# One AdaLN transformer block on one core: the second norm's chain and five engines' order within a step

## Chip, cores and metric

One NeuronCore of a Trainium2 chip (trn2) runs the whole program. The metric is device time in microseconds (us), of single executions; three of them are shown for the kernel before, with their median. One more execution was taken with the profiler, and all rows come from that one.

## What is computed

Eight batch rows of 1024 tokens with 256 channels go through two blocks, each with a layer norm, a modulation that depends on the row, and a gate on the residual. The first block is a causal linear attention over Chebyshev features, the second a mixture of eight experts with the top two chosen, plus one shared expert.

```python
def _layernorm(x, axis=-1, eps=1e-05):
    m = jnp.mean(x, axis=axis, keepdims=True)
    v = jnp.var(x, axis=axis, keepdims=True)
    return (x - m) / jnp.sqrt(v + eps)
...
    # attention: Tq, Tk are Chebyshev features of clipped q, k
    Tv = Tk * v[:, :, :, None, :]
    kv_prefix = jnp.cumsum(Tv, axis=2)
    ks_prefix = jnp.cumsum(Tk.sum(axis=-1), axis=2)
    num = (Tq * kv_beta).sum(axis=3)
    den = (Tq.sum(axis=-1) * k_beta).sum(axis=3)
    out_h = num / (den[..., None] + EPS_DEN)
    return jnp.einsum('bsd,ed->bse', out, W_out)
...
    # experts
    activation = jnp.sqrt(jax.nn.softplus(logits))
    top_vals, top_idx = jax.lax.top_k(activation, K)
    hdn = jax.nn.silu(jnp.einsum('nd,edh->enh', Xf, rW1) + rb1[:, None, :])
    y = jnp.einsum('enh,ehd->end', hdn, rW2) + rb2[:, None, :]
    routed = jnp.einsum('ne,end->nd', cf, y).reshape(B, T, d)
    return shared + routed
...
h = _layernorm(x, axis=-1) * (1 + ca) + sa
x = x + ga * _L0_attn_ref(h, L0_attn_W_in, L0_attn_W_out)
h = _layernorm(x, axis=-1) * (1 + cb) + sb
x = x + gb * _L0_ffn_ref(h, ...)
```

## The kernel before

The work is cut into 16 chunks of 512 tokens, two to a batch row: chunk (i, p) is half p of row i. The program is a software pipeline of steps, one per chunk, written out by hand for each engine (the `step` functions; a loop over rows 2 to 6 or 1 to 6, the first and last steps unrolled). In step (i, p) four chunks are in work at once: the first norm of the chunk two ahead, the query, key and value projections of the next chunk, the attention of chunk (i, p), the second norm and routing of the chunk before it (called prev), and the experts of the chunk two back. Each engine executes its list strictly in order, and semaphores join the lists.

The parts that the change and the prediction speak of, by engine:

- VectorE (`step` at L1191, in the block that begins at L957). `residual` (L1090) adds x to the output of W_out; `token_stats` (L368) takes the second norm's statistics with `bn_stats`; `odd` (L977) makes the third and fifth order features; `lows` (L961) makes a low part, the rounding rest of a normalised chunk, from PSUM, the high part and the modulation (n = 0 for the first norm, n = 1 for the second); `weigh` (L994) multiplies values by key features, `prefix` (L1010) is the prefix sum over tokens, `order_product` (L1032) multiplies by query features. Orders come in the sequence 0, 1, 3, 4, 2, so the fourth order product is that of order 4 and the fifth that of order 2. `logit_parts` (L1099) ranks the experts, `softplus` (L1126) and `combine_weights` (L1152) make the two weights of a token. `den_key_sums` and `den_products` make the denominators' terms, `invert` (L1069) takes the reciprocal, `finish_numerator` (L1076) adds the last order, `divide` (L1083) multiplies by the inverse that has been spread over the channels, and `weigh_hidden` (L1164) multiplies an expert's hidden layer by its weight.
- GpSimd (`step` at L738). `inv_std(pool, 1, ...)` (L346) turns the second norm's statistics into an inverse deviation and a shift, in ten small instructions. `weigh_order_5` (L648) makes the fifth order's weighted values; `scale_wo` (L716) scales W_out by the gate of the row, in p = 0 steps; `add_orders` (L655) issues a DMA that adds one order's product onto another in SBUF. The first (n = 0) waits for two order products, the second (n = 1) for four, the last (n = 2) for the landing of both. `exps` and `scores` are powers for the softplus and the square root, `split_weights` (L684) cuts the combine weights into bf16 parts.
- SyncE (`step` at L600) issues the other DMAs: `spread_inverse` (L572) writes the inverse denominators to DRAM (L576) and, when they are there, reads them back spread over the partitions (L581); `spread_weights` does the same for the combine weights; `load_gate` (L568) fetches a row's gate.
- ScalarE (`step` at L863): `highs` makes the high parts from PSUM, `normalise_second` applies the second norm, `scale_even` scales two query features, `copy_qkv` and `hidden` empty PSUM (the latter with SiLU), `combine_rows` copies the transposed combine weights.
- TensorE (`step` at L1503): `transposes`, `project`, `route_logits`, `logits_by_token`, `head_sums`, the nine experts, `denominators`, `project_out` (W_out) and `combine_by_expert`, the transposes of the combine weights.

What sets the order around the change is only the sequence of the calls in these five lists and the waits in front of each instruction. The last sum's wait is

```python
if n < 2:
    pool.wait_ge(products, ND * c + 2 * n + 2)
else:
    pool.wait_ge(added[0], 16 * c + 16)
    pool.wait_ge(added[1], 16 * c + 16)
```

## Time and profile before

| what | us |
|---|---|
| three runs | 957.63, 956.96, 951.9 |
| their median | 956.96 |
| the profiled execution | 953.07 |
| its span, first to last instruction | 951.3 |
| TensorE matmuls busy | 860.2 (90%) |
| VectorE busy | 815.7 (86%) |
| ScalarE busy | 489.8 (51%) |
| GpSimd busy | 408.3 (43%) |

Of the span, some 85 us are the setup and the first step, and the last 70 us are two steps with experts alone. In between the steps follow each other at 52 to 54 us. A timeline's row gives the start and the length of a group of like instructions, and in square brackets the idle time of the engine ahead of it with what ended that; an instruction that is much longer than its like was held while it ran.

### The profile page before, as it was taken

To read this page: it belongs to the slowest core of one execution; us is meant where nothing else is said; L and a number is where in the kernel's file an instruction comes from. 1 tells how busy PE (TensorE), PEld (TensorE's weight loads), DVE (VectorE), ACT (ScalarE), POOL (GpSimd) and SP (SyncE) were. 2 spreads that over 40 slices of the span, in tenths; PEclk is the share of its full clock that TensorE was granted. 3 is DMA by queue.
4 is the path that set the end of the run, shared out by engine and by line. 5 is a ranking of instruction groups with operands and counts; after the bars stand their busy time and mean duration, and the time that the engine had idled before them with its cause. 6 is when DMAs were issued, how large, how long until landed. Compare 5 with 4: busy or idle time off the path is not lost. (4 is left out here: it accounts for less than half of the span.)

```text
span 951.3 us, 14272 instructions
## 1 busy us (share of the span) xinstructions
PE 860.2 (90%) x4377; PEld 648.6 (68%) x4377; DVE 815.7 (86%) x1263; ACT 489.8 (51%) x860; POOL 408.3 (43%) x502
## 2 busy tenths in 40 slices
PE   5766739999999999999999999999999999979998
PEld 4545427676767676786767676777767676756786
DVE  2696979999989998999989998999999998889423
ACT  4634546555556656655656566566556563441321
POOL 2341444363636355453636254543646253463220
PEclk9975769999999999999999999999999999999999
DMA  8014134453533535453534445354634243443422
GB/s 309 1 29 89 45 68 145 86 153 76 137 92 77 153 79 160 86 155 70 153 77 96 130 87 165 68 155 90 162 71 133 66 100 113 78 133 83 117 79 55
DMA packets 51705, 100.34 MB, mean 105 GB/s; under 512 B 5380, under 2 KB 34127, under 8 KB 49623
## 3 DMA queue, kind: packets, MB, share of 16 engines
q1 hardware_dynamic: 36356, 66.14, 21.2%
q0 software_dynamic: 14832, 33.03, 20.2%
q10 hardware_dynamic: 482, 0.74, 0.2%
q8 instruction: 18, 0.29, 0.1%
q14 instruction: 17, 0.13, 0.0%
HBM read 57.68 MB, written 17.06 MB: 79 GB/s over the span
## 5 line engine op out<-in xcount | busy, mean ns | idle before, releaser
L1487 PE MATMUL acc<-w,hid 128*128 128x256 f32 x1128 | 262.5, 380 | 2.6 <-DVE hid L1169 2.6
L1487 PEld LDWEIGHTS acc<-w,hid 128*128 128x128 f32 x1128 | 213.9, 190 | 37.6 <-DVE hid L1169 4.7
L845 ACT ACTIVATE hid<-ring,b1row 128x512 f32<-128x512 f32 x144 | 98.7, 685 | 143.0 <-PE ring L1368 140.4
L1169 DVE TENSOR_TENSOR hid<-hid,cfw 128x512 f32<-128x512 f32 x128 | 111.1, 870 | 37.0 <-DMA cfw<-cf_rows 21.6
L665 POOL DMA_DIRECT2D feat<-feat x48 | 43.7, 910 | 228.8 <-DVE feat L1046 115.0
L800 ACT ACTIVATE feat<-ring,bqkv 128x512 f32<-128x512 f32 x96 | 65.7, 686 | 81.9 <-PE ring L1368 81.9
L1368 PE MATMUL ring<-n2H,w1H 128*128 128x512 f32 x288 | 102.5, 437 | 0.0
L1445 PE MATMUL tr<-wo_g,feat 128*128 128x256 f32 x256 | 65.3, 413 | 35.9 <-DVE feat L1088 35.9
L1021 DVE TENSOR_TENSOR_SCAN feat<-zero,carry,feat 128x512 f32<-128x512 f32 x80 | 97.1, 1261 | 0.0
L1021 DVE TENSOR_TENSOR_SCAN feat<-zero,feat 128x512 f32<-128x512 f32 x80 | 95.7, 1243 | 0.0
L1368 PE MATMUL ring<-n2H,w1L 128*128 128x512 f32 x288 | 90.8, 397 | 0.0
L1368 PE MATMUL ring<-n2L,w1H 128*128 128x512 f32 x288 | 90.5, 395 | 0.0
L1421 PE MATMUL tr<-feat,const 128*32 128x512 f32 x640 | 89.1, 602 | 0.0
L1445 PEld LDWEIGHTS tr<-wo_g,feat 128*128 128x128 f32 x256 | 51.6, 207 | 49.2 <-DVE feat L1088 33.7
L1368 PE MATMUL ring<-n1H,winH 128*128 128x512 f32 x192 | 69.5, 444 | 15.2 <-issue 7.9
L820 ACT ACTIVATE feat<-feat,const 128x1024 f32<-128x1024 f32 x64 | 70.2, 1142 | 1.0
L353 POOL TENSOR_TENSOR ms<-stats 128x4 f32<-128x4 f32 x18 | 30.2, 1678 | 88.4 <-DVE stats L378 88.4
L1368 PEld LDWEIGHTS ring<-n2H,w1L 128*128 128x128 f32 x288 | 54.4, 189 | 12.7
L1368 PEld LDWEIGHTS ring<-n2L,w1H 128*128 128x128 f32 x288 | 54.5, 189 | 12.5
L1368 PE MATMUL ring<-n1H,winL 128*128 128x512 f32 x192 | 62.8, 409 | 0.0
L1368 PE MATMUL ring<-n1L,winH 128*128 128x512 f32 x192 | 62.8, 409 | 0.0
L1368 PEld LDWEIGHTS ring<-n2H,w1H 128*128 128x128 f32 x288 | 48.8, 191 | 18.5 <-issue 11.7
(171 smaller groups left out, 1559.8 us busy)
## 6 DMA issues: line engine op xcount, KB each, us to landing
feat<-feat POOLq DMA_DIRECT2D x48, 512.0 KB, 4.6
cfw<-cf_rows SPq DMA_DIRECT2D x16, 1280.0 KB, 7.6
xin<-in_L_attn_x SPq DMA_DIRECT2D x16, 512.0 KB, 9.3
feat<-inv_rows SPq DMA_DIRECT2D x32, 256.0 KB
cfw<-cf_rows SPq DMA_DIRECT2D x16, 512.0 KB, 3.6
out<-x SPq DMA_DIRECT2D x15, 512.0 KB, 8.5
out<-fin POOLq DMA_DIRECT2D x15, 512.0 KB, 6.0
cfw<-cf_rows SPq DMA_DIRECT2D x16, 256.0 KB, 4.5
```

Of the source, the lines that this page charges most:

```text
L353: nc.gpsimd.tensor_tensor(t(1), m0, m1, ALU.subtract).then_inc(mv_steps[n], 1)
L665: g.dma_start(f(into), f(of), accum_op=ALU.add).then_inc(added[n], 16)
L800: a.activation(feat[:, (K0 + p, Q0 + p, V0)[m // 2], m % 2], ring[bank][:, :], ACT.Identity, bias=col(bqkv[:, (2, 3, 0, 1, 4, 5)[m]], i)). ...
L820: a.activation(f((qa, qb)[which - 1]), f(s), ACT.Square, bias=cv["biases"][:, which - 1:which]).then_inc(squares, 1)
L845: a.activation(hid[:, e % NG], ring[bank][:, :], ACT.Silu, bias=b1row[:, e:e + 1]).then_inc(ring_copied, 1)
L1021: last = v.tensor_tensor_scan(feat[:, W + n, h], zero[:, 0:1].to_broadcast([P, CT]), feat[:, W + n, h], carry[:, n, h:h + 1] if p else 0.0 ...
L1169: v.tensor_tensor(hid[:, e % NG], hid[:, e % NG], cfw[:, (e - 1) % NW], ALU.mult).then_inc(hidw_ready, 1)
L1368: last = mm(out, w, x, start=(n == 0), stop=(n == len(terms) - 1))
L1421: last = mm(tr[q][g_ * QS:(g_ + 1) * QS, :], cv["headsum"][:, (r // HPH) * QS:(r // HPH + 1) * QS], feat[:, srcs[n], h], start=(n < 4 and ...
L1445: last = mm(tr[t // 2][:, (t % 2) * D:(t % 2 + 1) * D], attn[:, k, t * P:(t + 1) * P], wo_g[:, k], start=(k == 0), stop=(k == KD - 1))
L1487: last = mm(acc[t // 2][:, t % 2], hid[:, e % NG, t * P:(t + 1) * P], w2[:, e], start=False, stop=(e == E), skip_group_check=True)
```

## The change

Every edit changes the order of calls, apart from the second norm's statistics, which get a new path. The lists in words:

- Second norm: VectorE finishes mean and variance itself (`bn_aggr` and two small instructions), and GpSimd keeps a power and a multiplication.
- VectorE: first low part right behind the statistics, second low part ahead of the first prefix sum, logit parts behind expert 3, softplus behind the denominators, combine weights ahead of the reciprocal.
- GpSimd: the order-5 product waits for the second weighted value; the powers of the routing move ahead of the second and of the last order sum, the first norm's inverse deviation to the end.
- ScalarE: the second norm's four normalisations and high part ahead of the key and query copies, the combine rows ahead of the first norm's normalisation.
- TensorE: the two norms' transposes, routing and token logits sooner, head sums later, the combine transposes ahead of W_out.
- SyncE: the gate for W_out is fetched at the end of the row before.

```diff
+        def second_mean_var(dve, i, p):
+
+            c = number(i, p)
+            dve.wait_ge(stats_ready[1], c + 1)
+            dve.sem_inc(aggregate_begun, 1)
+            for t in range(NT):
+                last = nc.vector.bn_aggr(mean_var[:, t], stats[:, 1, t])
+            last.then_inc(aggregated, 1)
+            dve.wait_ge(aggregated, c + 1)
+            nc.vector.tensor_scalar(ms[:, 1, 8], mean_var[:, :, 1], EPS_LN, None, ALU.add).then_inc(mean_var_ready, 1)
+            nc.vector.tensor_scalar(ms[:, 1, 10], mean_var[:, :, 0], -1.0, None, ALU.mult).then_inc(mean_var_ready, 1)
+
+        def second_inv_std(pool, i, p):
+
+            c = number(i, p)
+            pool.wait_ge(mean_var_ready, 2 * c + 2)
+            ge(pool, norm_ready[1], c)
+            nc.gpsimd.tensor_tensor(ms[:, 1, 9], ms[:, 1, 8], k_("-half", NT), ALU.pow).then_inc(second_pow, 1)
+            pool.wait_ge(second_pow, c + 1)
+            nc.gpsimd.tensor_tensor(ms[:, 1, 11], ms[:, 1, 10], ms[:, 1, 9], ALU.mult).then_inc(rstd_ready[1], 1)
...
             def step(i, p, gb, loads):
                 if p == 0:
-                    if loads or i < B:
-                        ge(sp, wo_ready, i)
-                        load_gate(i, 0)
+                    if i == 0:
+                        load_gate(0, 0)
...
+                if p == CB - 1 and i + 1 < B:
+                    sp.wait_ge(wo_ready, i + 1)
+                    load_gate(i + 1, 0)
...
                 ge(pool, numerator, c)
+                pool.wait_ge(weighted, (ND - 1) * c + 2)
                 g.tensor_tensor(f(W + 4), f(KT5), f(V0), ALU.mult).then_inc(weighted5, 1)
...
-                    inv_std(pool, 1, *later(i, p, -1))
+                    second_inv_std(pool, *later(i, p, -1))
...
-                if st["attn"]:
-                    add_orders(i, p, 1)
-                if st["norm"]:
-                    inv_std_of_squares(pool, *later(i, p, 2))
                 if st["second"]:
                     exps(*later(i, p, -1))
                 if st["attn"]:
+                    add_orders(i, p, 1)
+                if st["second"]:
+                    scores(*later(i, p, -1))
+                if st["attn"]:
                     add_orders(i, p, 2)
                 if st["second"]:
-                    scores(*later(i, p, -1))
                     split_weights(*later(i, p, -1))
+                if st["norm"]:
+                    inv_std_of_squares(pool, *later(i, p, 2))
...
                 silu(0)
-                silu(1)
                 if qkv:
                     highs(0, *nxt)
+                if second:
+                    for t in range(NT):
+                        normalise_second(act, *prev, t)
+                silu(1)
                 silu(2)
                 if attn_:
                     scale_even(i, p)
-                for t, half in enumerate(HALVES[:4]):
-                    copy(half)
-                    if second:
-                        normalise_second(act, *prev, t)
-                silu(3)
                 if second:
                     highs(1, *prev)
-                silu(4)
+                for half in HALVES[:3]:
+                    copy(half)
                 if second:
                     copy_logits(*prev)
+                copy("q1")
+                silu(3)
+                silu(4)
...
                 silu(8)
+                if second:
+                    combine_rows(*prev)
...
-                if second:
-                    combine_rows(*prev)
...
                     token_stats(dve, 1, *prev)
+                    second_mean_var(dve, *prev)
+                if qkv:
+                    lows(0, *nxt)
                 if attn_:
                     odd(i, p, 1)
                     weigh(i, p, 0)
-                if qkv:
-                    lows(0, *nxt)
+                    weigh(i, p, 1)
+                if second:
+                    lows(1, *prev)
...
-                if second:
-                    lows(1, *prev)
-                if attn_:
                     order_product(i, p, 0)
                     order_product(i, p, 1)
                 expert(3)
+                if second:
+                    logit_parts(*prev)
...
                     order_product(i, p, 2)
                     order_product(i, p, 3)
-                if second:
-                    logit_parts(*prev)
-                if attn_:
                     den_key_sums(i, p)
                     den_products(i, p)
+                if second:
+                    softplus(*prev)
...
                 expert(5)
                 if second:
-                    softplus(*prev)
+                    combine_weights(*prev)
                 if attn_:
                     invert(i, p)
...
                 if ffn:
                     expert_up(*exp, use, 0)
+                if qkv:
+                    transposes(0, *nxt)
+                if ffn:
                     expert_up(*exp, use, 1)
                     second_biases(*exp)
...
                 expert(0)
-                if qkv:
-                    for half in HALVES[:4]:
-                        project(*nxt, use, half)
-                expert(1)
                 if second:
                     transposes(1, *prev, behind_norm=qkv)
-                expert(2)
+                if qkv:
+                    for half in HALVES[:3]:
+                        project(*nxt, use, half)
                 if second:
                     route_logits(*prev)
+                if qkv:
+                    project(*nxt, use, "q1")
+                if second:
+                    logits_by_token(*prev)
+                expert(1)
+                expert(2)
...
                 expert(8)
+                if second:
+                    combine_by_expert(*prev, attn_)
...
                 if attn_:
                     project_out(i, p)
-                if second:
-                    combine_by_expert(*prev, attn_)
```

VectorE around the third and fourth order product, before, in step (7, 0); the same sequence stands in every step with both norms. L1008 is a weighted value, L1021 the prefix sums of two orders, L1169 expert 4, L1042 and L1046 the two order products, L1107 to L1113 the beginning of the logit parts:

```order
L1008 TENSOR_TENSOR feat<-feat 128x1024
L1021 SCALAR_TENSOR_TENSOR feat<-zero,feat 128x512 x4
L1169 TENSOR_TENSOR hid<-hid,cfw 128x512
L1030 COPY carry<-feat 128x4
L1042 TENSOR_TENSOR feat<-feat 128x1024
L1046 SCALAR_TENSOR_TENSOR feat<-feat 128x1024
L1107 TENSOR_REDUCE route<-misc 128x32
L1111 TENSOR_TENSOR prod<-route 128x256
L1113 MAX top<-route 128x8 x4
```

The same place after the change (lines are 30 higher there):

```order
L1147 SCALAR_TENSOR_TENSOR best<-top 128x8
L1149 TENSOR_SCALAR best<-top 128x8
L1152 TENSOR_TENSOR prod<-prod,const 128x256
L1154 TENSOR_REDUCE route<-prod 128x32
L1038 TENSOR_TENSOR feat<-feat 128x1024
L1051 SCALAR_TENSOR_TENSOR feat<-zero,feat 128x512 x4
L1199 TENSOR_TENSOR hid<-hid,cfw 128x512
L1060 COPY carry<-feat 128x4
L1072 TENSOR_TENSOR feat<-feat 128x1024
L1076 SCALAR_TENSOR_TENSOR feat<-feat 128x1024
L1086 SCALAR_TENSOR_TENSOR prod<-const,tr 128x512
```

The logit parts have moved from behind the two order products to ahead of the weighted value; the denominators' prefix sum (L1086) follows the products.

VectorE at the beginning of the same step, before: residual (L1096), statistics (L378), odd features (L984, L986), weighted values (L1002, L1004), first low part (n1L), prefix sums:

```order
L1096 TENSOR_TENSOR x<-tr,xin 128x512 x2
L378 BN_STATS stats<-x 128x6 x4
L984 SCALAR_TENSOR_TENSOR feat<-feat 128x1024
L986 SCALAR_TENSOR_TENSOR feat<-feat 128x1024
L1002 TENSOR_TENSOR feat<-feat 128x1024
L968 SCALAR_TENSOR_TENSOR n1L<-tr,mods,n1H 128x512 x2
L1004 SCALAR_TENSOR_TENSOR feat<-feat 128x1024
L1021 SCALAR_TENSOR_TENSOR feat<-zero,feat 128x512 x2
L1169 TENSOR_TENSOR hid<-hid,cfw 128x512
L1004 SCALAR_TENSOR_TENSOR feat<-feat 128x1024
L1169 TENSOR_TENSOR hid<-hid,cfw 128x512
L1021 SCALAR_TENSOR_TENSOR feat<-zero,feat 128x512 x2
```

And after it, to the second low part:

```order
L1126 TENSOR_TENSOR x<-tr,xin 128x512 x2
L381 BN_STATS stats<-x 128x6 x4
L390 BN_AGGR mean_var<-stats 128x2 x4
L393 TENSOR_SCALAR ms<-mean_var 128x4
L394 TENSOR_SCALAR ms<-mean_var 128x4
L998 SCALAR_TENSOR_TENSOR n1L<-tr,mods,n1H 128x512 x2
L1014 SCALAR_TENSOR_TENSOR feat<-feat 128x1024
L1016 SCALAR_TENSOR_TENSOR feat<-feat 128x1024
L1032 TENSOR_TENSOR feat<-feat 128x1024
L1034 SCALAR_TENSOR_TENSOR feat<-feat 128x1024
L998 SCALAR_TENSOR_TENSOR n2L<-tr,mods,n2H 128x512 x2
```

Before, the second low part stands one small copy behind these twelve rows, after two pairs of prefix sums, three weighted values and two experts; now only the aggregation, the first low part and four products lie between the statistics and it.

GpSimd from the order-5 product (L653) to the weights' split (L698), before. L723 is W_out's scaling, the L665 are the three order sums, L672 the power of the softplus, L681 the scores:

```order
L653 TENSOR_TENSOR feat<-feat 128x1024 [waits numerator,odd_ready]
L723 TENSOR_TENSOR wo_g<-wo,gates 128x512 [waits projected,ga_loaded]
L665 DMA feat<-feat 128x1024 [waits order_products] x2
L672 TENSOR_TENSOR best<-pool_c,best 128x8 [waits softplus_steps,logit_parts]
L665 DMA feat<-feat 128x1024 [waits orders_added0,orders_added1]
L681 TENSOR_TENSOR best<-best,pool_c 128x8 [waits combine_weight_steps,softplus_steps]
L698 TENSOR_TENSOR part<-split,pool_c 128x32 [waits combine_transposed,combine_weight_steps]
```

And after it:

```order
L680 TENSOR_TENSOR feat<-feat 128x1024 [waits values_weighted,numerator,odd_ready]
L750 TENSOR_TENSOR wo_g<-wo,gates 128x512 [waits projected,ga_loaded]
L692 DMA feat<-feat 128x1024 [waits order_products]
L699 TENSOR_TENSOR best<-pool_c,best 128x8 [waits softplus_steps,logit_parts]
L692 DMA feat<-feat 128x1024 [waits order_products]
L708 TENSOR_TENSOR best<-best,pool_c 128x8 [waits combine_weight_steps,softplus_steps]
L692 DMA feat<-feat 128x1024 [waits orders_added0,orders_added1]
L725 TENSOR_TENSOR part<-split,pool_c 128x32 [waits combine_transposed,combine_weight_steps]
```

The softplus power stands ahead of the second sum and the scores ahead of the last one; the order-5 product has one more wait.

## Rows read from the trace of the kernel before

**Rows 1.** Busy time by stretch, divide to divide: length, then each engine; clock, DMA.

```profile
403.16:455.02 51.86, 50.53 (x266) 38.46 (x266) 49.99 (x75) 30.19 (x55) 23.51 (x30) 1.00 0.45 112
...
455.02:508.31 53.29, 51.11 (x267) 38.38 (x267) 49.87 (x80) 30.48 (x57) 26.36 (x30) 1.00 0.46 114
```

**Rows 2.** VectorE's timeline, one p = 1 step: start, us, instructions, [idle before <-releaser].

```profile
413.82 1.41 DVE L968 SCALAR_TENSOR_TENSOR n1L<-tr,mods,n1H 128x512 fp32r<-128x512 f32 x2
...
418.65 2.83 DVE L1169 TENSOR_TENSOR hid<-hid,cfw 128x512 f32<-128x512 f32 x1
...
426.49 1.41 DVE L968 SCALAR_TENSOR_TENSOR n2L<-tr,mods,n2H 128x512 fp32r<-128x512 f32 x2 [0.91 <-ACT n2H L788]
...
438.26 1.21 DVE L1046 SCALAR_TENSOR_TENSOR feat<-feat 128x1024 f32<-128x1024 f32 x1
...
439.40 0.21 DVE L1107 TENSOR_REDUCE route<-misc 128x32 f32<-128x64 f32 x1
...
439.99 0.37 DVE L1113 MAX8 top<-route 128x8 f32<-128x8 f32 x4
...
441.45 1.28 DVE L1056 TENSOR_TENSOR_SCAN prod<-const,kcarry,tr 128x512 f32<-128x512 f32 x1
...
455.02 1.34 DVE L1088 TENSOR_TENSOR feat<-feat 128x512 f32<-128x512 f32 x2 [0.38 <-DMA feat<-inv_rows]
```

**Rows 3.** GpSimd's timeline, the same step.

```profile
414.84 1.04 POOL L363 TENSOR_TENSOR ms<-ms,pool_c 128x4 f32<-128x4 f32 x1
...
417.51 3.42 POOL L653 TENSOR_TENSOR feat<-feat 128x1024 f32<-128x1024 f32 x1
...
440.06 0.87 POOL L665 DMA_DIRECT2D feat<-feat  x1 [6.96 <-DVE feat L1046]
...
445.15 0.91 POOL L665 DMA_DIRECT2D feat<-feat  x1 [0.38 <-issue]
...
447.30 1.66 POOL L681 TENSOR_TENSOR best<-best,pool_c 128x8 f32<-128x8 f32 x1 [1.24 <-DVE best L1150]
```

**Rows 4.** SyncE's queue, the end of the same step.

```profile
447.88 0.62 SPq L576 DMA_DIRECT2D inv_rows<-denom  x1
...
450.06 1.21 SPq L581 DMA_DIRECT2D feat<-inv_rows  x2
```

**Rows 5.** GpSimd's timeline, the end of the last attention step (7, 1).

```profile
868.12 0.91 POOL L665 DMA_DIRECT2D feat<-feat  x1 [2.53 <-issue]
```

**Rows 6.** SyncE's queue there.

```profile
869.71 0.63 SPq L576 DMA_DIRECT2D inv_rows<-denom  x1
...
873.06 1.21 SPq L581 DMA_DIRECT2D feat<-inv_rows  x2
```

**Rows 7.** ScalarE's timeline in step (7, 1): SiLU, one of two scalings, four normalisations.

```profile
837.69 0.69 ACT L845 ACTIVATE hid<-ring,b1row 128x512 f32<-128x512 f32 x1 [1.57 <-PE ring L1368]
...
838.28 1.05 ACT L828 ACTIVATE feat<-feat 128x1024 f32<-128x1024 f32 x1
...
845.83 2.07 ACT L435 ACTIVATE ntok<-x,ms 128x256 f32<-128x256 f32 x4 [5.56 <-POOL ms L366]
```

**Rows 8.** VectorE's timeline, the next step (p = 0): expert 2, second low part.

```profile
472.42 2.67 DVE L1169 TENSOR_TENSOR hid<-hid,cfw 128x512 f32<-128x512 f32 x1 [0.26 <-DMA cfw<-cf_rows]
...
479.76 1.41 DVE L968 SCALAR_TENSOR_TENSOR n2L<-tr,mods,n2H 128x512 fp32r<-128x512 f32 x2 [2.22 <-ACT n2H L788]
```

**Rows 9.** GpSimd's timeline there: W_out's scaling.

```profile
479.56 1.29 POOL L723 TENSOR_TENSOR wo_g<-wo,gates 128x512 f32<-128x512 f32 x1 [5.02 <-DMA gates<-gate_rows]
```

**Rows 10.** TensorE's timeline: W_out of steps (7, 0) and (7, 1).

```profile
826.75 5.41 PE L1445 MATMUL tr<-wo_g,feat 128*128 128x256 f32 x16 [2.07 <-DVE feat L1088]
...
879.69 3.72 PE L1445 MATMUL tr<-wo_g,feat 128*128 128x256 f32 x16 [2.35 <-DVE feat L1088]
```

**Rows 11.** Busy time by stretch, the first of these two.

```profile
826.70:832.00 5.30, 5.25 (x16) 4.24 (x17) 4.07 (x6) 0.00 (x0) 1.57 (x2) 0.68 0.32 31
```

**Rows 12.** Who waited for whom: us in total, times, longest.

```profile
DVE n2L L968 <- ACT n2H L788: 24.8, 16, 3.6
```

22 lines of the change are left out of this document (9 added, 13 removed).

## Prediction

> **What bounds the kernel now.** I looked first at the stretches from one divide to the next, one step each. The two shown last 51.86 and 53.29 us; TensorE is busy for 50.53 and 51.11 us of them and VectorE for 49.99 and 49.87 [rows 1]. Two engines are full at once, so busy shares decide nothing and the question is which chain closes the loop. The step ending at 455.02 stands for a second half row (p = 1), the next for a first one (p = 0); the kernel has six of the one kind and seven of the other between the divides at 137.35 and 825.36, which last 52 to 54 us.
>
> Next I read VectorE's own timeline [rows 2]. The divide at 455.02 waited for the spread of the inverse denominators (0.38 us, DMA), so VectorE's own work is not what ends there. Following that wait back over three queues gives a chain with fixed links. The fourth order product (438.26) ends at 439.40. GpSimd issues the second order sum at 440.06, the last order sum at 445.15 [rows 3]; SyncE writes the inverse at 447.88, issues its spread at 450.06 [rows 4], and the spread lands as the divide starts at 455.02. So the divide comes 15.62 us after the fourth order product: 0.66 + 5.09 + 4.91 + 4.96.
>
> The third link is the one to look at twice: is it the small write that takes 2.18 us (447.88 to 450.06), or does the spread wait until the last sum is through? In the last attention step the last sum is issued at 868.12 [rows 5] and the write at 869.71, so the write is 1.2 us nearer to the sum than before; the spread goes at 873.06 [rows 6]. The write now took 3.35 us, and the distance from sum to spread is 4.94, the same as 4.91. I read this as: the write is held until the last sum has gone through. The second link is of the same kind: in the code the last sum waits for the second to land.
>
> The Trainium skill, DMA: Bandwidth & Descriptors, Queues, rings and completion order, says that each DMA engine goes round between the queues it has work for, packet by packet; by that rule a small write would not wait for a whole transfer from another queue. The same section says that a semaphore's increment lands only after all earlier writes of that engine across its queues, which is what the 3.35 us look like. The first rule is a rival below.
>
> **The change, part by part.** I count to the end of the fourth order product, which was 36.24 us after the divide (403.16 to 439.40), and add the chain behind it.
>
> What leaves VectorE ahead of that point in a p = 1 step: the wait for the second norm's high part, 0.91 us, and a stall: weighted values of order 5 on GpSimd (3.42 us at 417.51) held VectorE's product at 418.65 for 2.83 instead of the usual 0.68, so 2.15 [rows 2, 3]. The change makes GpSimd start that product only behind the second weighted value, so that it runs while VectorE waits for, or makes, the low part. Low parts read PSUM and were not held by GpSimd: the one at 413.82 took its 1.41 us beside GpSimd's power at 414.84, and the one at 426.49 as long. Together 3.06 us go. In the p = 0 step shown they are 2.22 for the high part and 0.26 + 1.99 at the held product [rows 8]: 4.47.
>
> What comes in ahead of that point. Four aggregations and two small instructions: no row shows the aggregation; four MAX of eight elements took 0.37 us together [rows 2], which bounds it below, and 1.5 would be four times as much; with two small ones I take 0.75, near the MAX. The logit parts move from behind the fourth product to ahead of it: 439.40 to 441.45, 2.05 us, and VectorE is in order, so every order product and both GpSimd sums behind them are that much later. Third, a wait at the low part, which now stands six instructions behind the statistics. Its chain from the statistics' end: 0.75, the power 1.04 and a multiplication on GpSimd with their hand-overs 1.4, four normalisations 2.07, two SiLU at about 0.6, two scalings of the query features (1.05 each, partly overlapped: 1.95), which ScalarE now does ahead of the high part, 0.65 for its first half: 8.1 us with the hand-overs [rows 3, 7]. VectorE has 0.75 + 1.33 + four products at 1.14 = 6.65 us to do meanwhile. Wait: 1.45; bounds 0 (ScalarE free sooner) and 2.9 (the power held up by VectorE's products, as GpSimd's small instructions were). For p = 0, W_out's scaling on GpSimd, 1.29 us at 479.56 [rows 9], which ran beside a low part, now follows the order-5 product and meets a prefix sum; I take 1.0, bounds 0 and 1.3.
>
> Behind that point the chain stays 15.62, plus what GpSimd adds: the scores' power (1.66 us at 447.30) now stands ahead of the last sum. Today it starts 5.85 us behind the logit parts (441.45 to 447.30), with two clips and a weighted product of about 0.6 each between, which now follow it; so it can start some 4 us behind the fourth product and ends 5.7 behind it, just as the second sum lands (0.66 + 5.09 = 5.75). I take 0.15 more; 0 to 0.6, which is one clip.
>
> Sum for p = 1: -3.06 + 0.75 + 2.05 + 1.45 + 0.15 = +1.3 us. For p = 0: -4.47 + 0.75 + 2.05 + 1.45 + 1.0 + 0.15 = +0.9. VectorE does less behind the point, but it then waits longer at the divide: work taken out there buys nothing.
>
> Six steps at 1.3 and seven at 0.9 make 14.1. The ends: step (0,0) has no second norm, but its first low part now stands ahead of four products and waits for the high part; 0 to 4 us, I take 1.5. Step (0,1) by the p = 1 sum: +1.3. Step (7,1) has the longest wait of all for the high part, 3.6 us [rows 12]. It has no first low part to fill the time, so the power stands behind a product (1 us more) and only 0.75 + 4.56 us of work lie beside a chain of 9.1: the wait comes back as 3.8, no stall goes, and 0.75 + 2.05 + 0.2 = +3.0 stay. The last two steps: the combine rows start earlier, against TensorE idle between transposes, routing and token logits; 0, bounds -2 and +2. All in all 14.1 + 1.5 + 1.3 + 3.0 = 19.9.
>
> Costed at nothing: TensorE's new order (it gains a wait of about 0.7 for a key copy that now follows the high part, but has 2 us to spare ahead of W_out); the combine transposes ahead of W_out (their GpSimd work follows the combine weights, which now end before the inverse is written, 7 us ahead of the divide); the gate's load a step sooner (GpSimd's next instruction waits for order products anyway); GpSimd's ten small instructions that become two (they end in the chain above).
>
> The profiled execution took 953.07 (span 951.3): 953.07 + 19.9 = 973.0. The median of the runs is 956.96, so a measured figure may lie up to 4 us higher.
>
> **Rivals.**
> The write is not held, by the round rule above. Then the spread follows the write by 2.18 us. The write moves from 8.48 to 7.2 us behind the fourth product (less 2.05, plus combine weights and their wait for the scores, 0.8), and the divide to 7.2 + 2.18 + 4.96 = 14.35, 1.4 less than my 15.77. Steps become -0.1 and -0.5, the ends 1.5 - 0.1 + 1.6; together -1: 952, no change. Against it stand the 3.35 us [rows 6]; for it, that in the loop's steps write and sum end so close together that they don't tell.
>
> Faster: the chain is free as above and VectorE's new wait of 1.45 does not come, because ScalarE has the high part ready. Then VectorE needs 36.24 - 3.06 + 0.75 + 2.05 + 14.35 = 50.3 us and TensorE becomes the bound, at about 50.8 + 0.5 = 51.25 for both kinds: -0.6 x 6 - 2.0 x 7 = -17.6, with 2 for the ends 937. It decides as soon as the divide leaves less than 14 us behind the fourth product. The busy 50.53 and 51.11 [rows 1] show that floor.
>
> Slower still: TensorE idles 2 to 3 us ahead of W_out in every step, and its clock drops. After 2.07 us of idle that product took 5.41 us at a granted clock of 0.68, towards the lower level of 1.2 GHz; after 2.35 us elsewhere it took 3.72 [rows 10, 11]. If it falls in each of 13 steps, the residual waits 1.5 more: 973 + 19 = 992.
>
> **How the numbers follow.** Forecast 973, chance 0.52, own range 960 to 985. No change (952) 0.22, faster (937) 0.16, clock (992) 0.10. The range of 943 to 986 leaves out the lower part of the third and the upper of the fourth. A measurement tells about 1% from no change: faster 0.2 (the third case and a little of the second), within 0.26, slower 0.54.
>
> **What would show it.** Right: the last sum to the spread stays at 4.9; the fourth product 37 us or more behind the divide; VectorE waiting about 2 us for the inverse's spread at each divide; the held product back to 0.68; a wait of 1 to 2 us at the second low part. Wrong: the spread following the write by 2.2 us with the last sum still under way, or steps at 51 us with TensorE never waiting ahead of W_out.

## The result, and the profile after

The changed kernel takes 991.1 us (median of four, 989.7 to 994.4) against 954.4 for the kernel before (median of four, 951.6 to 957.6): a ratio of 1.0388, with a 95% interval of 1.0338 to 1.0438. The forecast was 973 and its range ended at 986. The profiled execution took 994.4 us with a span of 992.7, so it can be set against the 951.3 of before stretch by stretch, though it was the slowest of the four. From the starts of the 16 divides in each trace (the last column is an experiment, below, and its profiled execution was the fastest of its four, so the last two columns lie further apart than the medians do):

| us | before | changed | a_warm6 |
|---|---|---|---|
| to the first divide | 84.4 | 90.0 | 85.5 |
| step (0, 1) | 53.0 | 52.5 | 51.7 |
| six p = 1 steps, mean | 52.0 | 53.8 | 53.4 |
| seven p = 0 steps, mean | 53.7 | 56.3 | 55.0 |
| step (7, 1) | 52.8 | 56.2 | 54.7 |
| behind the last divide | 73.1 | 76.8 | 73.9 |
| span | 951.3 | 992.7 | 970.7 |

Busy time by stretch in the changed kernel, one p = 1 step and the p = 0 step behind it (columns as in [rows 1]):

```profile
421.01:474.25 53.24, 51.01 (x266) 38.39 (x266) 48.76 (x82) 29.91 (x55) 19.65 (x21) 1.00 0.43 109
474.25:530.85 56.60, 53.37 (x266) 39.44 (x266) 50.02 (x85) 30.11 (x55) 21.09 (x22) 0.97 0.44 108
```

VectorE is busy for less of its step than before and the steps are longer: time went into waiting. TensorE's clock, 1.00 in both stretches of [rows 1], is 0.97 in the second. VectorE's timeline, for those two steps (the rows to 474.25 answer to [rows 2], the last two to [rows 8]):

```profile
428.46 0.38 DVE L390 BATCH_NORM_AGGREGATE mean_var<-stats 128x2 f32<-128x6 f32 x4 [0.15 <-DVE stats L381]
...
429.46 1.41 DVE L998 SCALAR_TENSOR_TENSOR n1L<-tr,mods,n1H 128x512 fp32r<-128x512 f32 x2 [0.35 <-ACT n1H L816]
...
436.50 1.41 DVE L998 SCALAR_TENSOR_TENSOR n2L<-tr,mods,n2H 128x512 fp32r<-128x512 f32 x2 [1.08 <-ACT n2H L816]
...
440.19 0.67 DVE L1199 TENSOR_TENSOR hid<-hid,cfw 128x512 f32<-128x512 f32 x1
...
447.74 0.22 DVE L1137 TENSOR_REDUCE route<-misc 128x32 f32<-128x64 f32 x1
...
457.25 1.22 DVE L1076 SCALAR_TENSOR_TENSOR feat<-feat 128x1024 f32<-128x1024 f32 x1
458.38 1.28 DVE L1086 TENSOR_TENSOR_SCAN prod<-const,kcarry,tr 128x512 f32<-128x512 f32 x1
...
474.25 1.29 DVE L1118 TENSOR_TENSOR feat<-feat 128x512 f32<-128x512 f32 x2 [1.96 <-DMA feat<-inv_rows]
...
481.15 0.69 DVE L1126 TENSOR_TENSOR x<-tr,xin 128x512 f32<-128x512 f32 x1 [1.50 <-PE tr L1475]
...
491.34 1.41 DVE L998 SCALAR_TENSOR_TENSOR n2L<-tr,mods,n2H 128x512 fp32r<-128x512 f32 x2 [1.41 <-ACT n2H L816]
492.67 3.29 DVE L1051 TENSOR_TENSOR_SCAN feat<-zero,feat 128x512 f32<-128x512 f32 x2
```

In these rows the fourth order product (457.25) ends at 458.38, 37.37 us behind the divide at 421.01, where [rows 2] had 36.24: 1.13 later. The four aggregations take 0.38, and the first low part waits 0.35. The expert's product at 440.19 takes 0.67 where one was held to 2.83 before. The second low part waits 1.08 us, and 1.41 in the p = 0 step, whose first pair of prefix sums is held to 3.29 us (the pair behind takes 2.33). The divide waits 1.96 us for the inverse's spread, where it waited 0.38. GpSimd's queue (answering to [rows 3]) and SyncE's (to [rows 4]) in the first of these steps:

```profile
435.58 2.40 POOL L680 TENSOR_TENSOR feat<-feat 128x1024 f32<-128x1024 f32 x1 [5.06 <-DVE feat L1034]
...
459.05 0.91 POOL L692 DMA_DIRECT2D feat<-feat  x1 [8.06 <-DVE feat L1076]
...
464.38 0.90 POOL L692 DMA_DIRECT2D feat<-feat  x1
```

```profile
465.71 0.63 SPq L600 DMA_DIRECT2D inv_rows<-denom  x1
469.30 1.21 SPq L605 DMA_DIRECT2D feat<-inv_rows  x2
...
483.04 0.68 SPq L593 DMA_DIRECT2D gates<-gate_rows  x1
```

The chain of the forecast stands: 458.38 to the second sum 0.67, to the last sum 5.33, to the spread 4.92, to the divide 4.95. The write of the inverse is now issued 1.33 us behind the last sum instead of 2.73, and its read still goes 4.92 behind that sum: 3.59 us after the write. TensorE's W_out behind a p = 0 and behind a p = 1 step (answering to [rows 10]):

```profile
422.44 3.72 PE L1475 MATMUL tr<-wo_g,feat 128*128 128x256 f32 x16 [2.32 <-DVE feat L1118]
...
475.59 5.41 PE L1475 MATMUL tr<-wo_g,feat 128*128 128x256 f32 x16 [2.10 <-DVE feat L1118]
```

Here is the part that was not in the sum. Both products waited some 2 us; one took 3.72 us and the other 5.41, and VectorE's residual waited 1.50 for it (481.15). Over the fast one (422.30 to 427.00) the granted clock was 1.00; in the second half of the slow one it was 0.60, near the lower of its two levels, 1.2 GHz (busy time by stretch, columns as in [rows 1]):

```profile
478.00:480.60 2.60, 2.60 (x8) 2.10 (x8) 1.66 (x2) 2.05 (x3) 0.86 (x1) 0.60 1.00 299
```

W_out took over 5 us eight times in this trace, against three times before, both counts with the two at the start. Who waited for whom over the whole run (us in total, times, longest), first the divide before the change, then the changed kernel:

```profile
DVE feat L1088 <- DMA feat<-inv_rows: 10.0, 12, 2.6
```

```profile
PE tr L1475 <- DVE feat L1118: 42.2, 16, 5.6
...
DVE feat L1118 <- DMA feat<-inv_rows: 37.2, 16, 4.7
...
DVE x L1126 <- PE tr L1475: 15.9, 14, 2.5
```

The divide's waits for the inverse's spread have grown from 10.0 to 37.2 us, and TensorE's waits for the divide, in the row above them, follow: in the loop each W_out now waits 1.7 to 3.3 us, where it waited 1.0 to 1.7. One p = 0 step (364.37 to 421.01) has a W_out of 3.72 us and is long all the same: its residual began 1.46 us late for a cause that the trace does not name.

### The profile page after: what moved, and what is told of

The parts are those of the page before. It is cut to its first block and busy times, and to the rows that moved or that the text cites. A ratio compares the mean times of both kernels' runs of the same rounds, so it can differ in the third digit from the quotient of the medians.

```text
span 992.7 us, 14221 instructions
## 1 busy us (share of the span) xinstructions
PE 877.4 (88%) x4377; PEld 656.9 (66%) x4377; DVE 808.6 (81%) x1359; ACT 483.8 (49%) x860; POOL 335.3 (34%) x374
## 5 line engine op out<-in xcount | busy, mean ns | idle before, releaser
L1517 PE MATMUL acc<-w,hid 128*128 128x256 f32 x1128 | 266.2, 381 | 7.7 <-DVE hid L1199 7.4
L1517 PEld LDWEIGHTS acc<-w,hid 128*128 128x128 f32 x1128 | 211.7, 190 | 49.8 <-DVE hid L1199 17.3
L1199 DVE TENSOR_TENSOR hid<-hid,cfw 128x512 f32<-128x512 f32 x128 | 86.4, 677 | 32.3 <-ACT hid L873 22.9
L1475 PE MATMUL tr<-wo_g,feat 128*128 128x256 f32 x256 | 73.3, 450 | 42.2 <-DVE feat L1118 42.2
L1398 PE MATMUL ring<-n2H,w1H 128*128 128x512 f32 x288 | 108.6, 458 | 0.0
L1051 DVE TENSOR_TENSOR_SCAN feat<-zero,feat 128x512 f32<-128x512 f32 x80 | 102.0, 1324 | 0.0
L1475 PEld LDWEIGHTS tr<-wo_g,feat 128*128 128x128 f32 x256 | 57.2, 229 | 56.2 <-DVE feat L1118 34.5
L1451 PE MATMUL tr<-feat,const 128*32 128x512 f32 x640 | 85.5, 596 | 0.0
L680 POOL TENSOR_TENSOR feat<-feat 128x1024 f32<-128x1024 f32 x16 | 39.2, 2448 | 86.1 <-DVE feat L1034 86.1
```

Source lines behind the costliest of these rows:

```text
L680: g.tensor_tensor(f(W + 4), f(KT5), f(V0), ALU.mult).then_inc(weighted5, 1)
L1051: last = v.tensor_tensor_scan(feat[:, W + n, h], zero[:, 0:1].to_broadcast([P, CT]), feat[:, W + n, h], carry[:, n, h:h + 1] if p else 0.0 ...
L1199: v.tensor_tensor(hid[:, e % NG], hid[:, e % NG], cfw[:, (e - 1) % NW], ALU.mult).then_inc(hidw_ready, 1)
L1398: last = mm(out, w, x, start=(n == 0), stop=(n == len(terms) - 1))
L1451: last = mm(tr[q][g_ * QS:(g_ + 1) * QS, :], cv["headsum"][:, (r // HPH) * QS:(r // HPH + 1) * QS], feat[:, srcs[n], h], start=(n < 4 and ...
L1475: last = mm(tr[t // 2][:, (t % 2) * D:(t % 2 + 1) * D], attn[:, k, t * P:(t + 1) * P], wo_g[:, k], start=(k == 0), stop=(k == KD - 1))
```

## The experiments

**Is it the clock?** Small products with constants are put on TensorE ahead of W_out's wait, so that it does not idle there; nothing uses them. This is the edit with six of them:

```diff
                 c = number(i, p)
+                for n in range(6):
+                    mm(tr[1][:, 0:P], ident, ident, start=True, stop=True)
                 pe.wait_ge(attn_ready, 2 * c + 2)
```

a_warm has 14 in their place:

> The changed kernel with 14 small matrix products (128 x 128, constants) on TensorE ahead of W_out's wait for the divide, into the PSUM bank that W_out then overwrites; they compute nothing that is used. Theory: the idle of 2.0 to 2.6 us ahead of W_out is what the clock falls on, so with about 1.5 us of it filled W_out takes 3.72 us in every step instead of 5.4 in six or seven of them, and the residual no longer waits: 7 x 1.6 = 11 less, 980. Rival (the fall has another cause, or costs nothing since the second low part waits anyway): 989 to 992.

It took 988.8, 1.0332 (1.0276 to 1.0388). TensorE's timeline (each product is two instructions there):

```profile
415.93 3.29 PE L1471 MATMUL tr<-const 128*128 128x128 f32 x28
419.06 3.62 PE L1477 MATMUL tr<-wo_g,feat 128*128 128x256 f32 x16
```

No W_out in the loop was slow, but the filling was too long: W_out began 2.3 us behind the start of the divide (416.75) instead of 1.4, and most of what the clock gave was lost again. a_warm6 has six:

> The changed kernel with 6 of the small products ahead of W_out instead of 14 (the 14 took 3.29 us and W_out began 1 us late behind them); again nothing uses them. Theory: 1.4 us of the idle are filled, W_out starts with the divide and takes about 3.7 us in every step, the two kinds of steps cost 53.3 and 55.0 us: 991 - 7 x 1.6 = 980. Rival (the clock's fall costs less than it shows, as the chain has other slack): 986 to 992.

It took 977.4, a ratio of 1.0265 (1.0234 to 1.0296) against the changed kernel's 1.0388: 1.2%, 12 us, come back for work that computes nothing. W_out starts 1.35 us behind its divide, where it started 1.34 behind in the changed kernel, so the gain is not an earlier start. TensorE's timeline, and VectorE's waits for W_out over the run (15.9 us in the changed kernel):

```profile
462.54 1.50 PE L1471 MATMUL tr<-const 128*128 128x128 f32 x12
464.75 3.72 PE L1477 MATMUL tr<-wo_g,feat 128*128 128x256 f32 x16 [0.71 <-DVE feat L1118]
```

```profile
  DVE x L1126: 5.4, 5
```

From the third step on no W_out is slow. Its p = 1 steps are 1.3 us longer than those of before, its p = 0 steps 1.3, and its span is 970.7.

**Do the logit parts ahead of the fourth product cost 2 us a step?** The one call moved in the kernel before:

```diff
                 expert(3)
+                if second:
+                    logit_parts(*prev)
                 if attn_:
                     weigh(i, p, 3)
...
-                if second:
-                    logit_parts(*prev)
```

> The kernel before with one call moved: the logit parts ahead of the last weighted value, as in the changed kernel. Theory: every one of 15 steps is 2.0 us longer, 954 + 30 = 984, and the divide waits about 2 us for the inverse's spread. Rival (what leaves VectorE behind the product pays for what comes ahead of it): 952 to 958.

It took 1022.4, 1.0712 (1.0659 to 1.0764): 68 us, over twice the theory's 30, and far from the rival. Alone, the call comes before its data. VectorE's timeline:

```profile
687.10 0.23 DVE L1107 TENSOR_REDUCE route<-misc 128x32 f32<-128x64 f32 x1 [2.63 <-PE misc L1402]
```

VectorE waited 2.63 us for the token logits and then spent the 2.05 us of the logit parts, and the fourth product came 4.7 us later (40.91 us behind the divide instead of 36.24). In the changed kernel, where the second norm's chain and TensorE's routing are earlier too, this wait is absent (447.74). The other way round, in the changed kernel:

```diff
-                if second:
-                    logit_parts(*prev)
...
                     order_product(i, p, 3)
+                if second:
+                    logit_parts(*prev)
...
-                if st["second"]:
-                    exps(*later(i, p, -1))
                 if st["attn"]:
                     add_orders(i, p, 1)
                 if st["second"]:
-                    scores(*later(i, p, -1))
+                    exps(*later(i, p, -1))
                 if st["attn"]:
                     add_orders(i, p, 2)
                 if st["second"]:
+                    scores(*later(i, p, -1))
```

> The changed kernel with the logit parts behind the fourth order product again, and GpSimd's two powers behind the second and the last order sum, as before. Theory (a fixed chain of 15.6 to 16.0 us from the end of the fourth product to the divide): that product ends 2.0 us sooner in the 15 steps that have both, so 991 - 30 = 961, and less idle ahead of W_out may save some clock falls of 1.6 each: 950 to 962. Rival (VectorE's total work or TensorE sets the step, and the place of the logit parts does not matter): 985 to 995.

It took 972.4, 1.0189 (1.0138 to 1.0239), 19 us less, not 30. VectorE's timeline of one p = 1 step:

```profile
551.36 1.21 DVE L1075 SCALAR_TENSOR_TENSOR feat<-feat 128x1024 f32<-128x1024 f32 x1
...
561.24 0.29 DVE L1187 SCALAR_TENSOR_TENSOR route<-route,best 128x32 f32<-128x32 f32 x2 [0.96 <-POOL best L708]
...
569.91 1.29 DVE L1117 TENSOR_TENSOR feat<-feat 128x512 f32<-128x512 f32 x2 [0.86 <-DMA feat<-inv_rows]
```

The fourth product ends at 552.50, 35.97 us behind the divide of that step, 1.4 sooner than in the changed kernel (35.3 to 36.1 over the p = 1 steps). But the combine weights (561.24) now wait for GpSimd's score, the reciprocal stands behind them, and the inverse is written 10.0 us behind the product instead of 7.3: the write has become the last thing. So I put the reciprocal ahead:

```diff
+                if attn_:
+                    invert(i, p)
                 if second:
                     combine_weights(*prev)
-                if attn_:
-                    invert(i, p)
```

> The changed kernel with the logit parts and both powers back as in a_logits_back, and the reciprocal ahead of the combine weights again. There the fourth product had come 1.9 us sooner but the step only 0.4 to 0.7, because the inverse was written 8.5 to 9.8 us behind that product and no longer 7.3. Theory: what held the write there was the combine weights' wait for GpSimd's score ahead of the reciprocal; without it the write goes 1.5 us or more sooner, the divide follows the fourth product by 15.7 again, steps of 51.3 to 52.9: 972 - 20 = 952. Rival (VectorE is simply full, whatever the order): 968 to 973.

976.2, 1.0231 (1.0203 to 1.0260): nothing won. The inverse was written 8.5 us behind the product instead of 10.0 and the divide waited for its spread in few steps, but the product itself came 1.9 us later, since the first low part now waited for its high part (VectorE's timeline):

```profile
534.01 1.41 DVE L997 SCALAR_TENSOR_TENSOR n1L<-tr,mods,n1H 128x512 fp32r<-128x512 f32 x2 [2.61 <-ACT n1H L815]
```

I put that down to the first norm's inverse deviation at the end of GpSimd's list, and put it back as well:

```diff
                     add_orders(i, p, 1)
+                if st["norm"]:
+                    inv_std_of_squares(pool, *later(i, p, 2))
...
-                if st["norm"]:
-                    inv_std_of_squares(pool, *later(i, p, 2))
```

> The kernel of a_invert_first with one more call put back: GpSimd's four instructions for the first norm's inverse deviation behind the second order sum instead of at the end of the step. In a_invert_first the first low part waited 2.6 us for the high part, since those four ran behind the split of the combine weights, 1.7 us into the next step. Theory: that wait goes, the fourth product ends 35.3 us behind the divide in p = 1 steps and 37 in p = 0, and the steps fall to 51.5 to 53.5: 976 - 25 = 951. Rival (VectorE and TensorE are full whatever the order, as the divide no longer waits): 968 to 978.

974.7, 1.0175 (1.0124 to 1.0226), far above the theory's 951. The wait at the low part shrank, to 1.48 us in the step at 521.31, and the two kinds of steps together by only 0.4 us. TensorE's timeline shows what was last, and its stretch from 515 the clock (columns as in [rows 1]):

```profile
513.10 2.50 PE L1517 MATMUL acc<-w,hid 128*128 128x256 f32 x8 [2.42 <-DVE hid L1198]
...
523.53 3.62 PE L1475 MATMUL tr<-wo_g,feat 128*128 128x256 f32 x16
```

```profile
515.00:518.00 3.00, 3.00 (x9) 2.37 (x8) 2.97 (x5) 0.88 (x2) 2.76 (x4) 0.52 0.20 67
```

W_out starts 2.2 us behind the divide at 521.31 without having waited for it, so TensorE itself is late: it had waited 2.42 us for a weighted hidden layer, and from 515 to 518 its granted clock was 0.52. Softplus and combine weights stood ahead of experts 5 and 6 on VectorE. Either that is the cause, or VectorE is full. All of the routing's tail went back, also GpSimd's part, the combine transposes (behind W_out again) and the combine rows; this is VectorE's part:

```diff
                 expert(5)
                 if second:
-                    combine_weights(*prev)
+                    softplus(*prev)
                 if attn_:
                     invert(i, p)
...
                 expert(8)
+                if second:
+                    combine_weights(*prev)
                 if attn_:
                     finish_numerator(i, p)
```

> The changed kernel with the whole tail of the routing as before: logit parts behind the fourth product, softplus behind expert 5, combine weights behind expert 8, GpSimd's powers, split and the first norm's inverse deviation, TensorE's combine transposes behind W_out and ScalarE's combine rows at the end of the step. What stays of the change is the second norm's chain forward, the order-5 product's wait and the gate's load. Theory A (in a_first_norm_back VectorE's softplus and combine weights stood ahead of experts 5 and 6, and TensorE waited 1.7 us for an expert's weighted hidden layer and came late to W_out): with the experts first again TensorE is in time, the fourth product ends at 35.2 and 36.8, the divide follows by 15.7 and the steps come to 51.3 and 52.6, 945 to 951. Theory B (VectorE is full with the wait of 1 us for the high part in its list): 52.5 and 53.7, 955 to 962.

953.4, 0.9967 (0.9933 to 1.0001). Steps of 51.2 to 52.4 (p = 1) and 52.6 to 52.9 (p = 0, but for the first and the last) are nearer to theory A, and the 21 us to a_first_norm_back support it, as do TensorE's waits for weighted hidden layers over the whole run, first in a_first_norm_back, then here:

```profile
PE acc L1517 <- DVE hid L1198: 25.7, 17, 2.4
```

```profile
PE acc L1517 <- DVE hid L1198: 2.4, 6, 0.5
```

The combine transposes, which moved with the rest, took TensorE 0.4 us ahead of W_out in the step shown and did not wait there, so they are the smaller part. The total lies a little above A's range, since the loop's gain is lost again at the ends (89.7 to the first divide, 76 behind the last). For the change it says: with the routing late, the second norm's chain forward is worth nothing that can be measured, and the whole loss comes in with the half that moves the routing forward.

**Smaller terms.** W_out's scaling ahead of the order-5 product:

```diff
+                    if p == 0 and not first:
+                        scale_wo(i)
                     weigh_order_5(i, p)
                     if first:
                         clip_gates()
-                    elif p == 0:
-                        scale_wo(i)
```

> The changed kernel with W_out's scaling on GpSimd ahead of the order-5 product instead of behind it. Theory: in p = 0 steps the first prefix sum behind the second low part falls from 3.29 us to 2.45, and what the scaling now holds (odd features, weighted values) only eats into the wait of 1.4 us for the high part: 7 x 0.9 = 6 us less, 985. Rival (the hold is moved and paid in full, since the order-5 product is later too): 991, no change.

995.7, 1.0432 (1.0370 to 1.0494): no gain, and a reason that neither theory had. GpSimd's timeline:

```profile
489.39 1.40 POOL L750 TENSOR_TENSOR wo_g<-wo,gates 128x512 f32<-128x512 f32 x1 [4.32 <-DMA gates<-gate_rows]
```

The gate had not landed. Its load is issued a step sooner in the code, but SyncE is in order, and it went out at 482.71 (483.04 in the changed kernel, the last row of SyncE's above), behind the weights' spread. The order-5 product without its new wait:

```diff
-                pool.wait_ge(weighted, (ND - 1) * c + 2)
                 g.tensor_tensor(f(W + 4), f(KT5), f(V0), ALU.mult).then_inc(weighted5, 1)
```

> The changed kernel without the order-5 product's wait for the second weighted value, so that GpSimd starts it about 2 us sooner, beside VectorE's weighted values. Theory (the product holds VectorE's instructions that read SBUF twice, by up to 2.1 us, of which the wait of 1.1 to 1.4 for the high part eats most): p = 1 steps 0.5 to 1 longer, p = 0 steps even, since W_out's scaling then no longer meets the prefix sum: 991 to 1000. Rival (the held product cost nothing and the new wait gains nothing): 988 to 992.

993.1, 1.0430 (1.0397 to 1.0464), within the theory's range, but its interval overlaps that of the changed kernel. With a W_out of 3.72 us ahead of them, its p = 1 steps take 54.0 (53.2 to 54.5, mean 53.8, in the changed kernel): the fourth product ends 38.15 us behind the divide instead of 37.37. In its p = 0 steps, 54.5 to 55.6 us, it ends at 38.55 instead of 38.84. The product's new wait pays 0.8 us in the one kind and costs 0.3 in the other, too little for the medians to show.

**Does the last sum hold the write?** Take the last sum's DMA away and let VectorE add:

```diff
-                dve.wait_ge(added[2], 16 * c + 16)
-                v.tensor_tensor(f(W), f(W), f(W + 2), ALU.add).then_inc(numerator, 1)
+                dve.wait_ge(added[0], 16 * c + 16)
+                dve.wait_ge(added[1], 16 * c + 16)
+                v.tensor_tensor(f(W + 4), f(W + 4), f(W + 2), ALU.add).then_inc(sum45, 1)
+                dve.wait_ge(sum45, c + 1)
+                v.tensor_tensor(f(W), f(W), f(W + 4), ALU.add).then_inc(numerator, 1)
```

> The changed kernel with the last order sum taken from GpSimd's DMA and made by VectorE with one more addition of 1.15 us ahead of the numerator. Theory (the small write of the inverse is held until the last sum's DMA is through): the spread now goes 2.0 to 2.2 us behind the write instead of 3.6 behind, and lands 4.95 later, so a step loses 1.2 to 1.5 us in spite of the addition: 991 - 15 x 1.3 = 971. Rival (the write takes its 3.6 us for its own reasons): the spread stays 3.6 behind the write, and the addition is hidden or paid: 991 to 1005.

964.1, 1.0108 (1.0084 to 1.0132), 27 us less than the changed kernel. SyncE's queue at the end of one p = 1 step, then VectorE's timeline of that step:

```profile
451.20 0.62 SPq L601 DMA_DIRECT2D inv_rows<-denom  x1
453.20 1.21 SPq L606 DMA_DIRECT2D feat<-inv_rows  x2
```

```profile
421.98 1.41 DVE L997 SCALAR_TENSOR_TENSOR n2L<-tr,mods,n2H 128x512 fp32r<-128x512 f32 x2 [1.43 <-ACT n2H L815]
...
456.52 1.21 DVE L1111 TENSOR_TENSOR feat<-feat 128x1024 f32<-128x1024 f32 x1
457.77 1.23 DVE L1113 TENSOR_TENSOR feat<-feat 128x1024 f32<-128x1024 f32 x1
459.12 1.29 DVE L1120 TENSOR_TENSOR feat<-feat 128x512 f32<-128x512 f32 x2
```

The read goes 2.00 us behind the write instead of 3.59, and the divide no longer waits: the two additions (456.52, 457.77) run straight into it. The gain of 27 us, against 20 in the theory, is not the sum's alone: TensorE's idle ahead of W_out fell to 1.2 to 1.8 us and no W_out behind the second was slow. Against a_warm6, whose W_outs are not slow either, it is 15 us by the two ratios, and the profiled steps are 0.3 (p = 1) and 0.7 us (p = 0) shorter, where the theory had 1.3.

That the sum holds the write can also be seen where the order of the two happened to turn round, in one step of a_warm (SyncE's queue, then GpSimd's timeline):

```profile
241.84 0.62 SPq L600 DMA_DIRECT2D inv_rows<-denom  x1
243.84 1.82 SPq L605 DMA_DIRECT2D feat<-inv_rows  x2
```

```profile
242.13 0.92 POOL L692 DMA_DIRECT2D feat<-feat  x1 [1.60 <-DMA feat<-feat]
```

The write was issued 0.29 us ahead of the last sum, and the read followed 2.00 us behind the write, with the sum just begun. A write issued 1.33 us behind the sum is held, this one was not.

In the kernel before the same edit gives:

> The kernel before with the last order sum made by VectorE. Theory (before, two chains end within 0.4 us of each other at the divide: the inverse's spread and VectorE's own list): the spread follows its write as before by 2.0 to 2.2, nothing is won there, and the addition of 1.15 us lengthens a step by 0.8 to 1.15: 954 + 14 = 968. Rival (only the chain over the last sum bounds the loop): 945 to 955.

974.4, 1.0165 (1.0109 to 1.0221). There VectorE's own list ended with the chain, so the addition was paid: 52.95 us against 51.9 in the p = 1 steps with a W_out of 3.72. TensorE's idle ahead of W_out rose to 1.9 to 2.5 us, and nine W_outs behind the second took over 5.

**A version that beats both.** In a_vector_sum VectorE is last, and the 1.43 us ahead of its second low part are paid. The order-5 product goes first on GpSimd, beside the residual (and without its wait for the second weighted value), then experts 1 and 2 on VectorE, moved up from behind the low part, fill the wait:

```diff
+                if st["attn"]:
+                    weigh_order_5(i, p)
                 if st["second"]:
                     second_inv_std(pool, *later(i, p, -1))
...
                     weigh(i, p, 1)
+                expert(1)
+                expert(2)
                 if second:
                     lows(1, *prev)
```

> The kernel of a_vector_sum with the order-5 product as GpSimd's first work of the step and without its wait for the second weighted value, so that it runs beside the residual, the statistics and the first low part. Theory (the residual, the statistics and the low parts are not held by it, since they read one SBUF operand): p = 1 steps stay at 52.9, p = 0 steps lose up to 0.9 of the held prefix sum: 958 to 964. Rival (the residual or the odd features are held by up to 2 us): 970 to 990.

> The same with experts 1 and 2 on VectorE ahead of the second low part. Theory: in a_vector_sum VectorE never waits at the divide, so the 1.2 to 1.4 us that it waits for the high part are paid in full, and two products of 0.6 us each fill them: 15 x 1.1 = 16 less than a_sum_order5, 943 to 948. Rival (the combine weights' spread or ScalarE's SiLU are not there that early, and the wait only moves): 955 to 964.

The first has only the edit on GpSimd and took 958.5, 1.0004 (0.9975 to 1.0034), within its theory's range, though the steps in the loop stayed at 52.9 and 54.1 and the scaling still meets a prefix sum (3.38 us at 577.02): what it gained lies mostly outside them, as in the 82.4 us to the first divide, which were 85.9. The second took 948.1, 0.9897 (0.9867 to 0.9928) against 958.9 in the same runs: 1% faster than the kernel before, and by the two ratios 4.7% faster than the changed one. The second low part now waits 0.21 us in a p = 1 step (516.64), where it waited 1.43. Busy time by stretch in the latter, two of its steps (columns as in [rows 1]):

```profile
500.90:552.58 51.68, 49.94 (x260) 37.84 (x261) 50.05 (x83) 29.92 (x54) 21.30 (x21) 1.00 0.40 103
552.58:606.18 53.60, 52.72 (x273) 38.92 (x271) 51.05 (x86) 30.14 (x55) 21.89 (x22) 1.00 0.39 104
```

Experts first need the combine weights early. The same edit on a_routing_back, whose weights come late:

> The same with the order-5 product first on GpSimd and experts 1 and 2 ahead of the second low part, as in a_sum_order5_experts, but with the last sum on GpSimd as before. Theory A: the wait for the high part is filled, 1 us less ahead of the fourth product, and TensorE's 51 us become the bound: steps of 51.2 and 52, 938 to 944. Theory B (the last sum's DMA holds the spread and its place decides): no less than a_routing_back, and more than the 948 of a_sum_order5_experts.

974.1, 1.0224 (1.0142 to 1.0305). Theory B's bound holds, but not its reason: the wait changed its place, to the two experts. VectorE's waits for the spread of the combine weights over the whole run (9.4 us in a_routing_back):

```profile
DVE hid L1198 <- DMA cfw<-cf_rows: 41.2, 17, 5.8
```

So the early routing, which costs the changed kernel its time, is what this order needs; it pays once the divide no longer hangs on the last sum.

## Why the prediction was wrong

**What held.** The chain from the fourth product to the divide: 15.87 us against the 15.77 forecast. The write held by the last sum: with the write 1.40 us nearer to the sum, sum to spread moved by 0.01, and without the sum's DMA, or with the write ahead of it, the read follows in 2.00. (In the forecast's own reading of the last step the write was 1.14 us nearer, not 1.2.) The Trainium skill says as much of the increment (DMA: Bandwidth & Descriptors, Queues, rings and completion order): it lands only after earlier writes of that DMA engine, across its queues; the traces agree: 3.59 us behind the sum, 2.00 without it. The rival "not held" falls with it, and the faster one too, which needed it. The terms ahead of the fourth product came to +1.13 us in a p = 1 step, against +1.19: aggregations and small ones 0.8 (0.75 in the sum), logit parts 1.9 (2.05), the second low part's wait 1.08 (1.45), the first one's 0.35 (not in it), and the stall of 2.15 gone. W_out's scaling cost 0.96 in the p = 0 step (1.0). So this p = 1 step grew by 1.38 us, as forecast; the six grew by 1.8 on average, two of them being about 1 us longer than the others.

**What failed.** Two steps. First, "Costed at nothing: TensorE's new order": the forecast counted the 2 us that TensorE has ahead of W_out as time to spare, and left the clock to a rival of 0.10. But it let the divide wait 2 us in every step, and W_out waits as long as the divide does. [rows 10] had two waits of that length; behind one W_out took 5.41, behind the other 3.72. One of two, over 13 steps and at 1.5 us, would have put some 10 us into the sum, and that rival near an even chance. The runs show the price: with the idle filled in a_warm6, 12 us come back, and the p = 1 and p = 0 steps, each 1.3 us longer than before, come near the 1.3 and 0.9 of the forecast. By the ratios (1.0209 forecast, 1.0388 measured) 17 us were missed. Two of the W_outs that a_warm6 shortens had been slow before the change too (138.70 and 826.75), some 3 us by their lengths, so about 9 of the 17 are the clock's.

That the clock rival's 992 is almost the measured figure is luck. It had a slow W_out in each of 13 steps; ahead of these steps five were slow, and one of the five had been slow before. The rest of the way was made up by the ends.

Second, the ends were mis-sized, in part by the same cause: +5.6 to the first divide where I took 1.5 with a bound of 4, -0.5 in (0, 1) where I took +1.3, +3.4 in (7, 1) where I took 3.0, +3.7 in the last two steps where I took 0 with a bound of 2. Together they are 12.2 us in the profiled execution, where I had 5.8. In the first step the low part waits 4.66 us for its high part, and behind the last divide TensorE waits 1.98 for the second one (VectorE's and TensorE's timelines):

```profile
45.79 1.60 DVE L998 SCALAR_TENSOR_TENSOR n1L<-tr,mods,n1H 128x512 fp32r<-128x512 f32 x2 [4.66 <-ACT n1H L816]
```

```profile
932.12 0.42 PE L1424 MATMUL misc<-n2H,rt 128*64 128x512 f32 x1 [1.98 <-ACT n2H L816]
```

The first of these is not a steady number: a_warm6, which leaves that step as it is, reached its first divide at 85.5, and other kernels with the same first step at 85.7 to 90.3.

In the p = 0 steps 0.9 was forecast, and the one with a quick W_out and no late residual (694.40 to 749.38, 54.98) shows 1.5 against the same step before (53.48); the seven differ by 2.6 on average, and the rest is a W_out of 5.3 to 6.3 us ahead of five of them and the late residual in one.

## What to carry to other kernels

Price a wait on every engine that takes part in it: two us at VectorE's divide were two us of TensorE idle, and in some steps the matmuls behind them took 1.7 us longer at the lower clock. Where a small transfer is on the path, look for the large one issued just ahead of it, from whatever queue; here taking that transfer away, and most of TensorE's idle with it, gave back 27 of 37 us. It paid only because the chain over that transfer ended last: in the kernel before, where VectorE's own list ended with it, the same edit cost 16 us. A call moved alone tells little (+68 us here), since what it needs must move with it; undo a change in halves that belong together, and each half then shows its price.

## What was not expected of the hardware

Idle time alone did not tell when TensorE's clock falls: of the W_outs ahead of the 13 steps the five slow ones all stood behind a p = 1 step, but of the seven that stand there two took 3.72 us, after 3.33 us of idle (365.72) and 2.33 (695.75), while the one at 475.59 took 5.41 after 2.10. In a_scale_early W_outs behind p = 0 steps were slow as well. What decides it is not shown. Six short products with constants ahead of W_out (twelve instructions, 1.50 us) were enough that it was not slow from the third step on. And GpSimd's order-5 product, which held VectorE's products with two SBUF inputs by 2 us before, ran in a_sum_order5_experts at 505.75 for 2.39 us beside the residual (505.57, PSUM and SBUF) without lengthening it (GpSimd's and VectorE's timelines there):

```profile
505.75 2.39 POOL L680 TENSOR_TENSOR feat<-feat 128x1024 f32<-128x1024 f32 x1 [0.33 <-DVE feat L1015]
```

```profile
505.57 1.30 DVE L1128 TENSOR_TENSOR x<-tr,xin 128x512 f32<-128x512 f32 x2
506.80 1.40 DVE L382 BATCH_NORM_STATS2 stats<-x 128x6 f32<-128x256 f32 x4
```
